# Second batch's weight rows handed over inside SBUF, late weight loads as steps of the first turns, new instruction orders

## Chip, cores and metric

The kernel runs on one core of one Trainium2 chip. The metric is device microseconds (us) of one execution; smaller is better.

## The reference, cut to what matters

Input x is 16 batches of 256 tokens by 256 channels. Four layers run one after the other on every batch, each steered by a 64-vector per batch:

```python
# A: adapter whose weights are generated per batch, then two norms and q, k, v
dW = (cond @ Wdd.T + bdd) * 0.1              # one 128x256 pair of matrices per batch
x  = x + relu(x @ (Wd + dWd).T + bd) @ (Wu + dWu).T + bu
x  = norm(x) * w + bias + tanh(...)          # layer 1
q, k, v = (norm(x) * g1 + b1) @ W_qkv.T      # layer 2, 16 heads of 16
# B: attention per head: softmax(q k^T / 4) v
# C: x + o @ W_o * a1;  then x + gelu_tanh(norm(x) @ W_f1) @ W_f2 * a2
# D: u = rms(x) @ up_w.T;  h = val * gelu(gate);  y = quant8(h) @ ternary(down_w).T + x
```

Batches do not depend on each other. The weights, and the generator of the adapter rows, are shared.

## The kernel before, in words

**Stages and turns.** The work of a batch is cut into stages A, B, C, D as above. In turn t the kernel does A of batch t, B of batch t-1, C of batch t-2 and D of batch t-3, so turns 0 to 18 cover 16 batches. The five instruction streams (SP issues every DMA; PE, ACT, DVE, POOL compute) are written out by hand: a text for each engine lists the order of the small steps ("A.v", "B.s0", "C.f1"), with `HEAD` for turns 0 to 5, `FULL` repeated for turns 6 to 12 and `TAIL` for the rest. Each step waits on semaphores that count the finished steps of other engines. An engine runs its own list strictly in order, so a step that waits holds all that stands behind it. PE is written `A.down, A.up, A.ht, A.q, A.k, A.v`; `B.s` are scores (each covers two of the eight head pairs), `B.m` the transposed maxima, `B.t` the transposed scores, `B.o` the outputs; `C.proj, C.ht, C.f0..3, C.g0..3, C.xt` are the output projection and the feed-forward; `D.u, D.qt, D.y` the last layer. Matmuls of A and C that need fp32 precision are done as three fp32r products of high and low parts (`three`, L504), hence every weight is split by ACT (`high_part`, L800) and DVE (`low_part`, L1040).

**Before the turns.** `hyper` (16 chunks of 1 MB, L344 and L370) streams through a ring of four buffers. PE turns each into rows of adapter weights for all 16 batches (L514), ACT and DVE in turn copy them into `gen` (L785, L981). As each chunk is ready SP copies the first batch's eight rows to `cur` (`first_rows`, L366). After the last one SP loads w_qkv (L399), stores all of `gen` to DRAM as `cur_scratch` in four transfers of 1 MB (L402), stores two constant planes (L404, L405), loads w_f1 (L408), waits for the four stores (L409), loads w_up (L410) over the place where it is split later, and starts the turns with `W.late` (w_f2 and w_down, L413 and L414). `gen` lies where the high part of w_up is written later.

**The adapter weights of a batch.** `combine(b)` on DVE (L1056, step `A.cur`) turns `cur` into `cur * 0.1 + base`. For b > 0 it waits for a load of `cur` from `cur_scratch` (L391), which SP issues in `A.load` together with the gates `tA` (L386) and the two layouts of x (L379, L380). In turn 0 DVE does `A.up A.lna A.lng A.ln W.qkv A.cur A.q`, so the q low part (L1132) stands behind `A.cur`, and PE's `A.v` (L504, twelve matmuls) waits for the q low part before it overwrites the bank.

**What else the steps touch.** `B.s0` of batch b needs the heads of q and k: ACT and DVE write high and low parts, SP stores them to `qk_scratch` (`A.qs`, `A.ks`, L420) and loads them back as heads 0 to 3 (`A.ql`, `A.kl`, L429). `C.g0` shares a bank with k and waits for the k low part (L1132). `C.f1` waits for the fourth maximum of stage B (L1140). DVE's `W.abs` (L1072) sums w_down.

The lines that cannot be said shorter, turn 0 and 1 of DVE:

```python
0: A.up A.lna A.lng A.ln W.qkv A.cur A.q 1: W.fa 0: A.k 1: A.up A.lna A.lng A.ln B.s0 B.s1 B.s2 B.s3 B.p0 B.m0
B.s4 B.s5 B.s6 B.s7 B.p1 B.m1 A.q W.up B.o1 A.k A.cur B.o3
```

Of the kernel before, what the change touches and what calls it, by code (L numbers as in the profile page):

```python
# [63 lines left out]
def at(steps, name, b):  # L64
# [13 lines left out]
        0: A.down A.up A.ht A.q A.k A.v 1: A.down A.up B.s0 B.s1 A.ht B.m0 B.s2 A.q B.s3 A.k B.m1 B.t0 B.t1 B.o0 B.t2 B.t3 B.o1 A.v 2: C.proj B.s0
# [1384 lines left out]
```

## Time and profile before

| | |
|---|---|
| time, median of 3 runs | 893.33 us (892.43 to 893.88) |
| time of the profiled execution | 892.32 us |
| its span, first to last instruction | 890.5 us |
| PE busy | 814.7 us, 91% |
| DVE, ACT, POOL busy | 551.0, 520.9, 235.1 us |
| all DMA engines busy (slices 2 and 4 of 40) | 382 and 409 GB/s |
| mean granted TensorE clock | 0.946 of full speed |
| chain that ended last, by engine | PE 80%, issue 8%, DVE 4%, DMA 3%, POOL 3% |

The span is shorter than the time by 1.8 us of start and end. Busy shares are means over stages of different kinds, so the views by stretch of time say more. A granted clock of 1.00 is 2.4 GHz and of 0.50 is 1.2 GHz.

### The profile page before, as it was taken

The numbers are of one execution on the slowest core, as the hardware profiler recorded it, in microseconds if no ns is written. First come the engines' busy times: TensorE is split into PE (matmuls) and PEld (weight loads), VectorE is DVE, ScalarE is ACT, GpSimd is POOL, SyncE is SP. The second block draws the span as 40 slices with busy tenths as digits, with TensorE's granted clock in tenths as the row PEclk, the third lists the DMA queues.
The fourth block names the chain that finished last, engine by engine and source line by source line (L and its number), as shares of the span: only waits on it lengthen the run. The fifth ranks groups of instructions, "written<-read, shape, count | busy, mean of one in ns | idle before, by whom it ended". The sixth has DMA issues, their size and how long they took to land.

```text
span 890.5 us, 15833 instructions
## 1 busy us (share of the span) xinstructions
PE 814.7 (91%) x5852; PEld 629.9 (71%) x5852; DVE 551.0 (62%) x1063; ACT 520.9 (58%) x808; POOL 235.1 (26%) x333
## 2 busy tenths in 40 slices
PE   6862477999999999999999999999999999999976
PEld 4212346777787878787878787878788787877665
DVE  1322567686767768585858585858585767656424
ACT  1112243566676758585867667666667676765642
POOL 1002213050505142423223140505050505030310
PEclk9855577999999999999999999999999999999999
DMA  9989733334242342424251514234242333230100
GB/s 346 382 309 409 234 130 112 117 113 150 71 163 72 110 135 85 160 85 161 84 162 52 178 64 151 94 117 129 102 139 102 119 114 107 102 101 3 31 13 12
DMA packets 56093, 118.48 MB, mean 133 GB/s; under 512 B 6000, under 2 KB 11504, under 8 KB 53312
## 3 DMA queue, kind: packets, MB, share of 16 engines
q1 hardware_dynamic: 56016, 117.48, 38.7%
q8 instruction: 46, 0.75, 0.3%
q14 instruction: 31, 0.25, 0.1%
HBM read 82.51 MB, written 34.16 MB: 131 GB/s over the span
## 4 chain that ended last, share of the span: by engine, by line
PE 80%; issue 8%; DVE 4%; DMA 3%; POOL 3%; ACT 1%; SPq 1%; POOLq 0%; DVEq 0%; ACTq 0%
PE bank L504 31%; PE bank L713 13%; PE pair_s L668 6%; PE pair_t L504 5%; PE bank L679 3%; PE bank L760 3%; PE pair_s L656 3%; PE pair_s L634 3%; DMA hyp<-in_hyper 2%; PE bank L572 2%; PE bank L578 2%; PE pair_t L656 2%; PE bank L752 2%; PE pair_t L634 1%; PE pair_t L514 1%
## 5 line engine op out<-in xcount | busy, mean ns | idle before, releaser
L713 PE MATMUL bank<-wf,G 128*128 128x256 f32 x512 | 126.6, 391 | 0.7 <-ACT G L885 0.5
L504 PE MATMUL bank<-wup_hi,hD_hi 128*128 128x512 f32 x256 | 110.2, 430 | 4.1 <-POOL hD_lo L1333 3.2
L1361 POOL TENSOR_TENSOR x<-x,xcr 128x512 f32<-128x512 f32 x16 | 20.8, 1301 | 335.4 <-DVE x L1198 335.4
L870 ACT ACTIVATE Pr<-pair_s 128x1024 f32<-128x1024 f32 x64 | 65.6, 1025 | 74.8 <-PE pair_s L656 74.8
L713 PEld LDWEIGHTS bank<-wf,G 128*128 128x128 f32 x512 | 92.2, 189 | 21.8 <-issue 5.8
L504 PE MATMUL bank<-wup_hi,hD_lo 128*128 128x512 f32 x256 | 101.6, 397 | 0.0
L504 PE MATMUL bank<-wup_lo,hD_hi 128*128 128x512 f32 x256 | 101.5, 396 | 0.0
L1140 DVE TENSOR_REDUCE nmax<-pair_s 128x4 f32<-128x1024 f32 x64 | 77.9, 1218 | 20.4 <-PE pair_s L634 20.3
L1164 DVE STREAM_TRANSPOSE oq<-pair_s 128x512 f32<-128x512 f32 x32 | 22.9, 717 | 88.7 <-PE pair_s L668 88.7
L1140 DVE TENSOR_REDUCE nmax<-pair_t 128x4 f32<-128x1024 f32 x64 | 77.4, 1210 | 0.0
L914 ACT ACTIVATE gl<-bank,rsD 128x512 f32<-128x512 f32 x64 | 43.8, 684 | 52.7 <-PE bank L504 52.5
L1208 DVE SCALAR_TENSOR_TENSOR hd<-bank,rsD,gl 128x512 f32<-128x512 f32 x64 | 47.8, 747 | 32.0 <-PE bank L504 30.8
L668 PE MATMUL pair_s<-Pr,Va 128*32 128x256 f32 x1024 | 65.1, 396 | 0.3 <-ACT Pr L870 0.2
L870 ACT ACTIVATE Pr<-pair_t 128x1024 f32<-128x1024 f32 x64 | 65.2, 1019 | 0.0
L504 PEld LDWEIGHTS bank<-wup_hi,hD_hi 128*128 128x128 f32 x256 | 48.3, 189 | 18.8 <-POOL hD_lo L1333 3.4
L504 PEld LDWEIGHTS bank<-wup_lo,hD_hi 128*128 128x128 f32 x256 | 48.4, 189 | 11.7
L504 PEld LDWEIGHTS bank<-wup_hi,hD_lo 128*128 128x128 f32 x256 | 48.6, 190 | 9.7
L668 PEld LDWEIGHTS pair_s<-Pr,Va 128*32 128x32 f32 x1024 | 29.6, 112 | 26.6 <-ACT Pr L870 8.4
L922 ACT ACTIVATE qT<-bank 128x1024 bf16<-128x1024 bf16 x32 | 32.8, 1024 | 23.6 <-PE bank L752 23.6
L504 PE MATMUL bank<-hA_hi,wqkv_hi 128*128 128x256 f32 x128 | 39.9, 312 | 3.4 <-POOL hA_lo L1333 3.4
L504 PE MATMUL bank<-hC_hi,wf_hi 128*128 128x256 f32 x128 | 38.1, 298 | 3.6 <-POOL hC_lo L1333 3.6
L1333 POOL TENSOR_TENSOR hA_lo<-hA,hA_hi 128x512 fp32r<-128x512 f32 x16 | 20.6, 1285 | 75.9 <-ACT hA_hi L849 75.9
(183 smaller groups left out, 2000.4 us busy)
## 6 DMA issues: line engine op xcount, KB each, us to landing
hyp<-in_hyper SPq DMA_DIRECT2D x16, 1024.0 KB, 8.6
Qp<-qk_scratch SPq DMA_DIRECT2D x64, 256.0 KB, 4.9
Kp<-qk_scratch SPq DMA_DIRECT2D x64, 256.0 KB, 4.7
qk_scratch<-q_hi SPq DMA_DIRECT2D x16, 512.0 KB, 2.8
qk_scratch<-k_hi SPq DMA_DIRECT2D x16, 512.0 KB, 3.4
tC<-rows_scratch SPq DMA_DIRECT2D x16, 384.0 KB, 4.3
xT_t<-in_xT SPq DMA_DIRECT2D x16, 256.0 KB, 4.3
x_t<-in_x SPq DMA_DIRECT2D x16, 256.0 KB, 4.5
```

Of the source, the lines that this page charges most:

```text
L504: mm = pe.matmul(dst, l, r, start=first and i == 0, stop=last and i == 2)
L634: mm = pe.matmul(pair[p % 2][:, half, r * L:(r + 1) * L], Qp[lo:lo + KR, 1 - par, p, r * P:(r + 1) * P], Kp[lo:lo + KR, 1 - par, p, :], st ...
L656: mm = pe.matmul(pair[p % 2][:, half, k * L:(k + 1) * L], Kp[lo:lo + KR, 1 - par, p, k * P:(k + 1) * P], Qp[lo:lo + KR, 1 - par, p, :], st ...
L668: mm = pe.matmul(bank[1][32 * j:32 * j + 32, (g % 2) * L:(g % 2 + 1) * L], Va[:, 1 - par, k, 4 * g + j, :], Pr[:, (2 * g + j // 2) % 4, j ...
L679: mm = pe.matmul(bank[5][:, r * D:(r + 1) * D], oT[:, k, r * P:(r + 1) * P], wo[:, k, :], start=k == 0, stop=k == KT - 1)
L713: mm = pe.matmul(bank[5][:, r * D:(r + 1) * D], G[:, k, r * P:(r + 1) * P], wf2[:, k, :], start=k == 0, stop=k == FT - 1)
L760: mm = pe.matmul(bank[6][:, 0:D], qT[:, k, :], wq3[:, k, :], start=k == 0, stop=k == FT - 1)
L870: act.activation(Pr[:, p % 4, :, :].rearrange("p a n -> p (a n)"), pair[p % 2][:, :, :].rearrange("p a n -> p (a n)"), ACT.Exp, scale=DH * ...
L914: act.activation(gl[:, n % 2, :], bank[6][:, :], ACT.Gelu, scale=rsD[:, 1, n // 2:n // 2 + 1]).then_inc(act_d, 1)
L922: act.activation(qT[:, :, :].rearrange("p k n -> p (k n)"), bank[7][:, :].bitcast(BF16), ACT.Copy).then_inc(act_d, 1)
L1140: dve.tensor_reduce(nmax[:, n % 2, :, p % GP, :], pair[p % 2][:, :, :].rearrange("p a (r n) -> p a r n", r=RT), AX.X, ALU.max, negate=True ...
L1208: dve.scalar_tensor_tensor(hd[:, (n % 2) * HALF:(n % 2 + 1) * HALF], bank[7][:, :], rsD[:, 1, n // 2:n // 2 + 1], gl[:, n % 2, :], ALU.mul ...
```

## The change

Four edits. (1) `first_rows` issues a second transfer for each chunk: the rows of batch 1 go from `gen` to a new SBUF tensor `second`, and `combine(1)` reads it, after PE's `A.up` of batch 0, which is the last reader of `cur`. The load of `cur` in `A.load` of turn 0 is dropped; that of turn 1 waits for the stores of `gen`. (2) w_qkv is loaded before the last four `first_rows`, not after them. (3) The stores and late loads become steps: `W.store` and `W.f` open turn 0, `W.up` stands behind `A.kl2` of turn 0, `W.late` behind `B.m0` of turn 1. The wait for all preparation before w_f1 is gone. (4) All five orders are new. The arithmetic is the same.

```diff
 HEAD = {
     "SP": """
-        0: W.late A.load A.qs A.ks A.ql0 A.kl0 A.ql1 A.kl1 A.kl2 A.kl3 A.ql2 A.ql3 1: A.load B.m0 A.qs B.m1 A.ql0 A.ql1 A.ks 2: C.tc 1: A.kl0 A.ql2
+        0: W.store0 W.f0 A.load A.qs A.ks A.ql0 A.ql1 A.kl0 A.kl1 A.ql2 A.kl2 W.up A.kl3 A.ql3 2: C.tc 1: A.load B.m0 W.late B.m1 A.qs A.ks A.ql0
...
     "PE": """
-        0: A.down A.up A.ht A.q A.k A.v 1: A.down A.up B.s0 B.s1 A.ht B.m0 B.s2 A.q B.s3 A.k B.m1 B.t0 B.t1 B.o0 B.t2 B.t3 B.o1 A.v 2: C.proj B.s0
-        A.down A.up B.s1 C.ht C.f0 C.f1 C.f2 W.abs B.m0 A.ht B.s2 C.f3 B.s3 A.q A.k B.m1 B.t0 A.v C.g0 B.t1 C.g1 B.o0 C.g2 B.t2 C.g3 B.t3 3: A.down
+        0: A.down A.up A.ht A.q A.k A.v 1: A.down A.up B.s0 B.s1 B.m0 A.ht B.s2 B.s3 A.q A.k B.m1 B.t0 B.t1 B.o0 B.t2 B.t3 B.o1 A.v 2: C.proj A.down
+        A.up B.s0 C.ht B.s1 W.abs C.f0 C.f1 C.f2 B.m0 A.ht B.s2 C.f3 B.s3 A.q A.k B.m1 B.t0 A.v C.g0 B.t1 C.g1 B.o0 C.g2 B.t2 C.g3 B.t3 3: A.down 2:
...
     "ACT": """
-        0: A.down W.qkv A.lnb A.ht W.fa A.q A.k A.v 1: A.down W.up A.lnb A.ht A.q A.k B.t0 B.t1 B.t2 B.t3 B.t4 B.t5 B.t6 B.t7 A.v 2: A.down C.lnb
+        0: W.qkv A.down A.lnb A.ht A.q A.k A.v W.fa 1: A.down A.lnb A.ht W.up A.q B.t0 B.t1 B.t2 B.t3 A.k B.t4 B.t5 B.t6 B.t7 A.v 2: A.down C.lnb
...
     "DVE": """
-        0: A.up A.lna A.lng A.ln W.qkv A.cur A.q 1: W.fa 0: A.k 1: A.up A.lna A.lng A.ln B.s0 B.s1 B.s2 B.s3 B.p0 B.m0 B.s4 B.s5 B.s6 B.s7 B.p1 B.m1
-        A.q W.up B.o1 A.k A.cur B.o3 2: C.proj B.s0 C.ln B.s1 A.up B.s2 A.lna A.lng B.s3 A.ln W.abs B.p0 B.m0 B.s4 B.s5 B.s6 B.s7 B.p1 B.m1 A.q A.k
+        0: W.qkv A.cur A.up A.lna A.lng A.ln A.q A.k 1: A.up A.lna A.lng A.ln B.s0 B.s1 B.s2 B.s3 B.p0 B.m0 W.fa B.s4 B.s5 B.s6 B.s7 B.p1 B.m1 A.q
+        A.cur W.up B.o1 A.k 2: W.abs 1: B.o3 2: C.proj C.ln A.up B.s0 A.lna B.s1 A.lng B.s2 B.s3 A.ln B.p0 B.m0 B.s4 B.s5 B.s6 B.s7 B.p1 B.m1 A.q
...
 FULL = {
     "SP": """
-        -1: A.kl2 A.ql1 A.kl3 A.ql2 A.ql3 D.y1 0: A.load B.m0 A.qs B.m1 D.y0 A.ks A.ql0 A.kl0 1: C.tc 0: A.kl1""",
+        -1: A.ql0 A.kl0 0: C.tc -1: A.kl1 D.y1 A.kl2 A.ql1 A.ql2 A.ql3 A.kl3 0: A.load B.m0 A.qs B.m1 D.y0 A.ks""",
     "PE": """
-        -1: B.m1 A.v B.t0 C.g0 B.t1 C.g1 D.qt1 B.o0 C.g2 B.t2 C.g3 B.t3 D.y1 B.o1 C.xt 0: A.down B.s0 C.proj D.u0 A.up D.u1 C.ht B.s1 D.u2 C.f0 C.f1
-        C.f2 B.m0 A.ht C.f3 B.s2 D.u3 B.s3 A.q D.qt0 A.k D.y0""",
+        -1: B.m1 A.v B.t0 C.g0 B.t1 C.g1 B.o0 D.qt1 C.g2 B.t2 C.g3 B.t3 D.y1 B.o1 C.xt 0: A.down B.s0 C.proj D.u0 A.up D.u1 C.ht B.s1 D.u2 C.f0 C.f1
+        C.f2 B.m0 C.f3 A.ht B.s2 D.u3 B.s3 A.q D.qt0 A.k D.y0""",
...
     "DVE": """
-        -1: C.g3 D.y1 B.o3 0: B.s0 C.proj B.s1 C.ln D.u0 A.up A.lna D.u1 A.lng B.s2 A.ln B.s3 B.p0 D.quant0 B.m0 D.u2 B.s4 B.s5 D.u3 B.s6 B.s7 B.p1
-        A.q A.k B.m1 D.quant1 A.cur D.y0 B.o1""",
+        0: D.u1 A.lng B.s2 B.s3 A.ln B.p0 D.quant0 B.m0 D.u2 B.s4 B.s5 D.u3 B.s6 B.s7 B.p1 A.q B.m1 A.cur A.k D.quant1 D.y0 B.o1 C.g3 D.y1 B.o3 1:
+        B.s0 C.proj B.s1 C.ln D.u0 A.up A.lna""",
     "POOL": """
-        0: A.down C.proj C.ln A.up C.ht A.lna A.ln A.ht C.g3 C.xt""",
+        0: A.ht C.g3 1: A.down 0: C.xt 1: C.proj C.ln A.up C.ht A.lna A.ln""",
...
+        second = staged("second", [P, 2 * D], F32, 2 * D)
...
                 sp.wait_ge(gen_act if c % 2 == 0 else gen_dve, c // 2 + 1)
                 sp.dma_start(cur[8 * c:8 * c + 8, :], gen[0:P:NB, c, :]).then_inc(first_in, 16)
+                sp.dma_start(second[8 * c:8 * c + 8, :], gen[1:P:NB, c, :]).then_inc(second_in, 16)
...
             def load_weights(b):
 
+                if b == 1:
+                    load_gates(b)
+                    return
                 sp.dma_start(cur[:, :], cur_rows[:, bass.ds(b, 1), :].rearrange("r o n -> (r o) n")).then_inc(cur_in, 16)
                 load_gates(b)
 
             load_rows(0)
+            sp.dma_start(wqkv_raw[:, :], w_qkv).then_inc(wqkv_in, 16)
             for c in range(NCH - 4, NCH):
                 first_rows(c)
             sp.wait_ge(rows_out, 16)
             load_gates(0)
-            sp.dma_start(wqkv_raw[:, :], w_qkv).then_inc(wqkv_in, 16)
...
-            sp.wait_ge(prep, len(PREP))
-            sp.dma_start(wf1_raw[:, :], w_f1).then_inc(wf1_in, 16)
-            sp.wait_ge(gen_out, 64)
-            sp.dma_start(wup_raw[:, :], w_up).then_inc(wup_in, 16)
+            def f1_rows():
+                sp.dma_start(wf1_raw[:, :], w_f1).then_inc(wf1_in, 16)
+
+            def up_rows():
+                sp.wait_ge(gen_out, 64)
+                sp.dma_start(wup_raw[:, :], w_up).then_inc(wup_in, 16)
...
                     elif (stage, what) == ("A", "load"):
 
+                        if t == 1:
+                            sp.wait_ge(gen_out, 64)
...
                 if b == 0:
                     dve.wait_ge(first_in, 16 * NCH)
+                elif b == 1:
+                    dve.wait_ge(second_in, 16 * NCH)
+                    dve.wait_ge(pe_a, at(PE_A, "up", 0))
                 else:
-                    dve.wait_ge(cur_in, 16 * b)
+                    dve.wait_ge(cur_in, 16 * (b - 1))
                 dve.wait_ge(dve_w, at(DVE_W, "base", 0))
-                dve.scalar_tensor_tensor(cur[:, :], cur[:, :], DELTA, base_c[:, :], ALU.mult, ALU.add).then_inc(cur_ready, 1)
+                dve.scalar_tensor_tensor(cur[:, :], second[:, :] if b == 1 else cur[:, :], DELTA, base_c[:, :], ALU.mult, ALU.add).then_inc(cur_ready, 1)
```

## Rows read from the trace of the kernel before

**Rows 1.** By stretch: length, busy PE, PEld, DVE, ACT, POOL; granted clock, DMA share, GB/s

```profile
57.00:60.00 3.00, 0.00 (x0) 0.00 (x0) 1.51 (x3) 0.00 (x0) 1.46 (x1) 0.50 0.16 49
...
83.00:86.00 3.00, 0.55 (x5) 0.34 (x3) 0.00 (x0) 0.84 (x2) 0.00 (x0) 1.00 0.96 401
84.00:93.00 9.00, 0.00 (x0) 0.00 (x0) 0.77 (x2) 0.43 (x2) 0.00 (x0) 0.62 0.97 366
...
140.00:150.00 10.00, 4.77 (x30) 3.17 (x29) 9.54 (x18) 4.50 (x7) 6.08 (x10) 0.88 0.00 1
...
185.00:850.00 665.00, 661.24 (x4979) 530.67 (x4978) 458.08 (x896) 450.89 (x700) 199.51 (x278) 1.00 0.33 107
850.00:890.50 40.50, 28.79 (x163) 22.59 (x161) 11.58 (x21) 12.07 (x20) 3.42 (x4) 0.96 0.04 14
```

**Rows 2.** Who waited for whom, 55 to 150 us: total, times, longest

```profile
DVE cur L1056 <- DMA cur<-cur_scratch: 20.2, 1, 20.2
...
PE bank L504 <- DVE q_lo L1132: 10.2, 1, 10.2
```

**Rows 3.** SP's DMA issues in time (start, length), and one group's min/median/max

```profile
58.70 0.43 SPq L399 DMA_DIRECT2D wqkv_raw<-in_w_qkv  x1
59.17 5.85 SPq L402 DMA_DIRECT2D cur_scratch<-gen  x4
...
76.14 0.33 SPq L410 DMA_DIRECT2D wup_raw<-in_w_up  x1
...
L366 SPq DMA_DIRECT2D cur<-gen x16: 563/580/725, 9.7 to 57.6; - x16
```

**Rows 4.** Timeline of turn 0 on DVE, POOL and ACT: start, length, instruction

```profile
67.16 0.19 POOL L1301 TENSOR_TENSOR rsA<-mvA,eps_ln 128x2 f32<-128x2 f32 x1 [7.86 <-DVE mvA L1099]
...
70.10 1.97 DVE L1040 TENSOR_TENSOR wqkv_lo<-wqkv_raw,wqkv_hi 128x1536 fp32r<-128x1536 f32 x1
70.41 1.71 POOL L1301 TENSOR_TENSOR rsA<-mvA,eps_ln 128x2 f32<-128x2 f32 x1
...
79.78 1.91 ACT L800 ACTIVATE wf_hi<-wf_raw 128x2048 fp32r<-128x2048 f32 x1 [2.56 <-DMA wf_raw<-in_w_f]
...
92.84 0.87 DVE L1132 SCALAR_TENSOR_TENSOR q_lo<-bank,small,q_hi 128x256 fp32r<-128x256 f32 x2
```

**Rows 5.** Chain of waits: PE pieces at the low and the high clock

```profile
93.76 2.94 PE bank L504 x12
...
100.08 2.09 PE bank L578 x4
...
199.78 1.42 PE bank L504 x12
```

**Rows 6.** Timeline: when batch 1's x had landed

```profile
94.65 2.38 POOL L1315 TENSOR_TENSOR x_t<-x_t,bu_t 128x512 f32<-128x512 f32 x1 [16.10 <-DMA x_t<-in_x]
```

**Rows 7.** Timeline of turn 1 on DVE and PE

```profile
93.62 2.28 DVE L1040 TENSOR_TENSOR wf_lo<-wf_raw,wf_hi 128x2048 fp32r<-128x2048 f32 x1
...
102.19 0.69 DVE L1106 TENSOR_TENSOR x<-bank,x_t 128x512 f32<-128x512 f32 x1 [5.50 <-PE bank L578]
...
112.45 0.28 DVE L1154 CAST mt<-pair_s 32x128 fp32r<-32x128 f32 x1 [0.49 <-PE pair_s L640]
...
117.58 1.23 DVE L1140 TENSOR_REDUCE nmax<-pair_s 128x4 f32<-128x1024 f32 x1 [1.51 <-PE pair_s L634]
...
121.15 0.50 PE L656 MATMUL pair_s<-Qp,Kp 64*128 64x256 f32 x4 [0.46 <-DVE mt L1154]
...
121.72 4.40 DVE L1040 TENSOR_TENSOR wup_lo<-wup_raw,wup_hi 128x4096 fp32r<-128x4096 f32 x1
...
127.83 0.72 DVE L1164 STREAM_TRANSPOSE oq<-pair_s 128x512 f32<-128x512 f32 x1 [1.71 <-PE pair_s L668]
```

**Rows 8.** Timeline of a middle turn, around the k low part

```profile
443.74 0.27 PE L640 MATMUL pair_s<-small,parts 128*32 128x128 f32 x1
...
443.84 0.88 DVE L1132 SCALAR_TENSOR_TENSOR k_lo<-bank,small,k_hi 128x256 fp32r<-128x256 f32 x2 [0.84 <-ACT k_hi L856]
...
446.03 1.35 PE L713 MATMUL bank<-wf,G 128*128 128x256 f32 x5
```

More of the change, by code:

```diff
@@ L77 @@
+        A.kl0 A.ql1 A.kl1 A.ql2 A.kl2 A.ql3 A.kl3 2: A.load B.m0 A.qs B.m1 A.ks A.ql0 A.kl0 A.ql1 3: C.tc 2: A.kl1 A.ql2 A.kl2 A.kl3 A.ql3 3: A.load
+        B.m0 A.qs B.m1 D.y0 A.ql0 A.ql1 A.ks A.ql2 A.kl0 A.kl1 4: C.tc 3: A.kl2 A.ql3 4: A.load 3: A.kl3 4: B.m0 A.ks B.m1 A.qs A.kl0 3: D.y1 4:
+        A.ql0 5: C.tc 4: A.kl1 D.y0 D.y1 A.ql1 A.kl2 A.ql2 A.kl3 A.ql3 5: A.load B.m0 A.qs B.m1 D.y0 A.ks""",
     "PE": """
[L78 removed]
@@ L101 @@
+        A.up C.ht A.lna A.ln A.ht C.g3 6: A.down 5: C.xt 6: C.proj C.ln A.up C.ht A.lna A.ln""",
 }
@@ L122 @@
+        D.y1 A.kl2 A.ql1 A.ql2 A.ql3 A.kl3 14: A.load B.m0 A.qs B.m1 D.y0 A.ks A.ql0 A.kl0 A.ql1 15: C.tc 14: D.y1 A.ql2 A.ql3 A.kl1 A.kl2 A.kl3 15:
+        B.m0 A.qs B.m1 D.y0 A.ks A.ql0 A.kl0 A.kl1 16: C.tc 15: A.ql1 A.kl2 A.kl3 D.y1 A.ql2 A.ql3 16: B.m0 B.m1 D.y0 D.y1 17: C.tc D.y0 D.y1 18:
+        D.y0 D.y1""",
     "PE": """
-        12: B.m1 A.v B.t0 C.g0 B.t1 C.g1 D.qt1 B.o0 C.g2 B.t2 C.g3 B.t3 D.y1 B.o1 C.xt 13: A.down B.s0 C.proj D.u0 A.up D.u1 C.ht B.s1 D.u2 C.f0
-        C.f1 C.f2 B.m0 A.ht C.f3 B.s2 D.u3 B.s3 A.q D.qt0 A.k D.y0 B.m1 A.v B.t0 C.g0 B.t1 C.g1 D.qt1 B.o0 C.g2 B.t2 C.g3 B.t3 D.y1 B.o1 C.xt 14:
@@ L398, in _, with store_rows @@
             load_gates(0)
-            sp.dma_start(wqkv_raw[:, :], w_qkv).then_inc(wqkv_in, 16)
-            for i in range(4):
-                sp.dma_start(cur_scratch[4 * i:4 * i + 4].rearrange("c p n -> p c n"), gen[:, 4 * i:4 * i + 4, :]).then_inc(gen_out, 16)
-            sp.wait_ge(zero, 6)
-            sp.dma_start(qk_scratch[0, :, 3, :], ys[:, :, :].rearrange("p r n -> p (r n)")).then_inc(planes_out, 16)
-            sp.dma_start(qk_scratch[1, :, 3, :], Kp[:, 1, 0:2, :].rearrange("p c n -> p (c n)").bitcast(F32)).then_inc(planes_out, 16)
-            sp.wait_ge(prep, len(PREP))
-            sp.dma_start(wf1_raw[:, :], w_f1).then_inc(wf1_in, 16)
-            sp.wait_ge(gen_out, 64)
-            sp.dma_start(wup_raw[:, :], w_up).then_inc(wup_in, 16)
+            def store_rows():
+                for i in range(4):
+                    sp.dma_start(cur_scratch[4 * i:4 * i + 4].rearrange("c p n -> p c n"), gen[:, 4 * i:4 * i + 4, :]).then_inc(gen_out, 16)
+                sp.wait_ge(zero, 6)
+                sp.dma_start(qk_scratch[0, :, 3, :], ys[:, :, :].rearrange("p r n -> p (r n)")).then_inc(planes_out, 16)
+                sp.dma_start(qk_scratch[1, :, 3, :], Kp[:, 1, 0:2, :].rearrange("p c n -> p (c n)").bitcast(F32)).then_inc(planes_out, 16)
+            def f1_rows():
[3 more added lines that the diff above has]
+                sp.dma_start(wup_raw[:, :], w_up).then_inc(wup_in, 16)
             def late_weights():
@@ L441, in turn @@
                     if stage == "W":
-                        late_weights()
+                        {"store": store_rows, "f": f1_rows, "up": up_rows, "late": late_weights}[what]()
                     elif (stage, what) == ("A", "qs"):
```

81 lines of the change are left out of this document (39 added, 42 removed).

## The prediction

> **What bounds the kernel now.** I read the busy time by stretch first [rows 1]. From 185 to 850 us PE is busy for 661.2 of 665 us at the full clock: turns 3 to 16 are PE's own work. An order that moves other engines about can win at most the 3.8 us of idle time there, and can only lose more if it makes PE wait. The idle time lies at both ends. At the start, 84 to 93 us has no matmul at all while the DMA engines are 97% busy, and 140 to 150 us has PE busy for half. At the end, 850 to 890.5 us is 11.7 us idle.
>
> Then the waits [rows 2]. PE waited 10.2 us in one piece, for the q low part of batch 0. That is a cheap instruction (0.87 us [rows 4]), held in DVE's list behind `combine(1)`, which itself waited 20.2 us for `cur` from `cur_scratch`. SP's issues say why that load is late [rows 3]: w_qkv and four 1 MB stores of `gen` go out from 58.7 us, SP waits until 76.14 us for the stores, then w_up, w_f2 and w_down (4 MB) are issued ahead of `cur`. So 4 MB of late weights stand between a finished row in `gen` and its use, and PE pays for it. This wait is what the change takes away.
>
> **The change, part by part.** Instants are those of the old trace; a minus is earlier.
>
> *Row transfers.* Sixteen more issues at 0.58 us [rows 3] on SP, one for each chunk. SP's loop has room: a chunk takes some 2.6 us, of which SP used about 1. The ring of chunks is DMA-bound, so what counts is the added traffic: 16 KB beside 1 MB is 1.6%, some 0.6 us over the loop of 45 us. Bounds: 0, and 1.3 us if eight rows keep only half of the engines busy. I take +0.6.
>
> *w_qkv earlier.* It now stands ahead of the last rows of batch 0. Between 57 and 60 us the DMA engines are 16% busy [rows 1], so most of its 0.8 MB (1.9 us at some 400 GB/s, the table's rate of full DMA engines) fills a hole, and the hole is where the last `cur` rows land. Bounds 0 and 1.9; I take +0.3, because the rows are issued about when it is nearly through.
>
> *combine(1).* It stands ahead of `A.up` on DVE and waits for the same PE step, so all of it is on the path: +0.7 (a 128x512 element pass on DVE is 0.69 us, `x` in [rows 7]).
>
> *W.qkv on DVE.* It used to start at 70.10 us, and POOL's 128x2 add at 70.41 took 1.71 us where the same add took 0.19 at 67.16 [rows 4]. Now it runs while PE does `A.down`, and POOL is free: -1.5. The Trainium skill (SBUF — State Buffer, section "SBUF: two separate sides") says that a DVE operation with two SBUF inputs and a GpSimd operation exclude each other for a whole instruction; the trace agrees, as the add ended with the DVE pass (72.1). The same rule speaks against the new place of `W.fa`, which now meets POOL's `hA_lo` of turn 1: there it could delay that subtraction by up to the pass's 2.28 us [rows 7]. I count nothing, since PE's `A.q` is by then held by other work (below).
>
> Together turn 0 reaches `A.q` at +0.6 +0.3 +0.7 -1.5 = +0.1.
>
> *The wait.* The q low part now follows q at once, some 83.5 us, when PE ends k: -10.2 for `A.v` [rows 2]. Beside that, PE's clock had gone to 1.00 by 83 us and fell while PE was idle: the mean over 84 to 93 is 0.62 [rows 1]. `A.v` will run without a gap behind k: twelve matmuls take 1.42 us at 2.4 GHz and 2.94 at 1.2 [rows 5], so -1.5. `A.down` gains nothing, as ACT now does `W.fa` (1.91 us [rows 4]) ahead of its relu. `A.up` (2.09 us [rows 5]) may halve or not: 0 to -1.0, I take -0.5. The x0 of batch 1, at 102.19 us before, comes at about 90.
>
> *Is the data there?* The x of batch 1 landed at 94.6 us [rows 6], behind the late weights. It is now issued some 72 us, behind 6.5 MB counted from 59 us; at 400 GB/s that is 78 us and with latency about 80 to 82. PE wants it at 85.6. Slack 4. Of the moved transfers w_up is issued behind six head loads at 90 us and ahead of the last two; ACT wants it at 100, and the heads behind it are wanted at 104, some 6 us after they land. w_f2 and w_down go out near 102 and are wanted at 118 or later. Stores of q and k find a short queue. All this I cost at nothing; the cover is the slack named.
>
> *Turn 1, DVE and PE.* Before, x0 to the first transposed score took 121.15 - 102.19 = 19.0 us [rows 7]. DVE now has `W.fa` (2.28 us) between the first maxima and pair 4. It used to wait 0.98 there and 1.51 before pair 6, because `A.q` stood ahead of `B.s3` on PE [rows 7]; so DVE's own chain does not grow. But PE now does `A.q` and `A.k` after `B.s3`, hence after the maximum of pair 5: 10.5 (the copy of the first maxima ends at 112.73 [rows 7]) + 2.3 (`W.fa`) + 2.4 (pairs 4, 5) + 0.8 = 16.0; `A.q` at the low clock 2.9, `A.k` at the high 1.4, then 0.9 for the maxima: 21.2. That is +2.2. Bounds: +0.8 with both at 2.4 GHz, +3.7 with both at 1.2. `W.up` (4.40) follows with `A.cur` ahead of it; DVE idled 1.71 before the output transpose at 127.83 [rows 7], so 0.69 more fits.
>
> *Turn 2.* `W.abs` leaves the busiest stretch of DVE (9.54 of 10 us in 140 to 150 [rows 1]) for one where DVE waits. In exchange `C.ln` comes ahead of `B.s0` and waits for POOL with DVE idle, so the fourth maximum, for which `C.f1` waits, is about as late as before: +0.3 (0 to +1).
>
> *The middle.* PE's work is the same and fills the time: 0, at best -0.5. *The end:* in turn 17 `C.ht` comes ahead of `D.u2`; that saves one short wait and adds another, and the last 27 us are one chain of the same steps: 0, bounds -1 and +1.
>
> Sum: 0.1 - 10.2 - 1.5 - 0.5 + 2.2 + 0.3 = **-9.6 us**. The profiled execution took 892.32 us, so 882.7; the median of the runs is 1.0 above it, which gives 883.7. I say 883.2.
>
> **The rivals.**
>
> *More than that (879.5).* The clock, once up at 83 us, stays up through turn 1, so that `A.up`, the scores and `A.q` run at 2.4 GHz: -0.5 and -1.5 and some in `B.o`, together -13. For it: PE's longest hole is gone. Against it: in the old trace the clock fell inside turn 1 as well, between score groups, and those gaps stay.
>
> *Less than that (887).* Another wait takes over in turn 1: the heads, or x of batch 1 behind the stores. If the 6.5 MB move at 320 GB/s instead of 400, they end 4 us later, the slack is used up, and a further 1 to 2 us are lost; with `A.k` at the low clock (+1.5) and 1.9 for w_qkv ahead of the first rows, the gain shrinks to 5 or 6.
>
> *Hidden anyway (893).* The change does not do what it says if something as late as `cur` stands behind it in turn 1. For that, the heads of batch 0 would have to be 10 us late again; but they were stored and loaded in 8 us, and only after the q low part.
>
> *Slower (899).* One mechanism: the k low part in every middle turn. It now stands behind `B.m1` and `A.cur` on DVE, while PE's `C.g0` waits for it. In the middle turn PE's maxima end at 444.01 us, then 0.2 + 0.6 + 0.9 puts the k low part at 445.8, and `C.g0` starts at 446.03 [rows 8]. The margin is 0.25 us in each of ten turns. The gain of 9.6 is eaten when it is overrun by 1 us in each; 899 needs 1.6. Against it: every length in that sum is a row, and DVE has idle time in each turn.
>
> **How the numbers follow.** Forecast (-8 to -12) 0.60; more 0.13; less 0.19; hidden 0.04; slower 0.04. A measurement of this kernel can tell about 0.2%, or 1.8 us. Faster by over 0.2%: 0.92; within: 0.04; slower: 0.04. The range 879 to 888 holds the forecast, most of "more" (low bounds of the clock terms) and most of "less".
>
> **What would show it.** No wait of DVE on `cur` in turn 0; `A.v` at about 83.5 us with the clock at 1.00; POOL's add near 0.2 us; x0 of batch 1 near 90; the first transposed score of batch 0 near 111; `C.f0` near 140 instead of 149.5; then 185-to-850-like PE busy of over 99%. Wrong: PE waits of over 2 us on heads or x in turn 1, a wait of `C.g0` on the k low part that recurs in each turn, or the chunk loop ending more than 1.5 us later.

## The result, and the profile after

The changed kernel took **890.17 us** (median of 20 runs, 888.61 to 892.01); the kernel before, run beside it, 891.84 (20 runs). The ratio is 0.9978, with a 95% interval of 0.9968 to 0.9988: a gain of 2 us where 9.6 were forecast, and the time lies outside the range. The profiled execution took 888.86 us, with a span of 887.0 at a mean granted clock of 0.948.

First who waited for whom in the changed kernel, 56 to 100 us (total, times, longest), to be held against [rows 2]:

```profile
POOL rsA L1316 <- DVE mvA L1114: 20.0, 2, 10.1
ACT x L844 <- POOL rsA L1323: 16.8, 2, 9.2
DVE q_lo L1147 <- ACT q_hi L868: 10.8, 1, 10.8
```

DVE's 20.2 us for `cur` and PE's 10.2 us for the q low part are gone. What DVE waits for now is ScalarE's q, the next step of the chain. One wait is new: PE starts the scores of batch 0 at 95.82 us, after 2.93 us of waiting for its heads, and over 2 us was a sign of being wrong in the prediction. It costs little, since DVE was busy with the norms of batch 1 meanwhile and takes the first maximum 4.8 us behind x0 in both kernels. The same is seen in the timeline of DVE and POOL in turn 0, against [rows 4] and [rows 7]:

```profile
63.86 0.69 DVE L1071 SCALAR_TENSOR_TENSOR cur<-cur,base_c 128x512 f32<-128x512 f32 x1 [2.99 <-DMA cur<-gen]
...
69.47 0.69 DVE L1071 SCALAR_TENSOR_TENSOR cur<-second,base_c 128x512 f32<-128x512 f32 x1 [3.25 <-issue]
...
75.17 0.19 POOL L1316 TENSOR_TENSOR rsA<-mvA,eps_ln 128x2 f32<-128x2 f32 x1
...
85.75 0.88 DVE L1147 SCALAR_TENSOR_TENSOR q_lo<-bank,small,q_hi 128x256 fp32r<-128x256 f32 x2 [10.81 <-ACT q_hi L868]
...
92.93 0.69 DVE L1121 TENSOR_TENSOR x<-bank,x_t 128x512 f32<-128x512 f32 x1 [3.74 <-PE bank L590]
```

Batch 1's rows are combined at 69.47 us, as soon as PE's `A.up` of batch 0 is through, without a wait for data; POOL's add is 0.19 us and no longer 1.71, and x0 of batch 1 comes at 92.93 where it came at 102.19: 9.3 us earlier. So the middle of the argument holds. The stretches of [rows 1] show that it does not hold at either end:

```profile
57.00:60.00 3.00, 1.94 (x8) 0.20 (x8) 0.42 (x1) 0.15 (x1) 0.00 (x0) 0.50 0.91 357
...
84.00:93.00 9.00, 7.15 (x36) 6.06 (x35) 1.82 (x5) 4.43 (x7) 0.71 (x1) 0.81 0.61 214
...
185.00:850.00 665.00, 659.72 (x4973) 527.73 (x4972) 450.37 (x879) 456.20 (x704) 194.17 (x269) 1.00 0.33 106
850.00:887.00 37.00, 26.13 (x131) 19.64 (x128) 11.67 (x21) 9.48 (x15) 3.42 (x4) 0.85 0.04 15
```

84 to 93 us, empty before, now has PE busy for 7.15 us. But at 57 to 60, where the chunk loop was over, PE still does the last chunk's eight matmuls with the DMA engines 91% busy. And the last stretch has the clock at 0.85, not 0.96. The chain of waits shows how far the loop slipped:

```profile
57.57 1.98 PE pair_t L526 x8
...
60.29 3.37 DMA cur<-gen
...
63.86 0.70 DVE cur L1071
...
64.70 1.52 PE bank L584 x3
```

In the kernel before, the same four pieces start at 54.89, 57.61 (and take 1.87), 59.67 and 60.51 us. The first matmul of the turns is **4.2 us later**, where the prediction had 0.9.

The table gives marks of every kernel of this study, from the profiled execution of each: the start of the last chunk's matmuls (L), the first matmul of `A.down` of turns 0, 1 and 3 (D0, D1, D3), the time from D3 to D5, and from `A.down` of turn 15 to the end of the span (E). "Change" is the ratio of the medians.

| kernel | median us | change [95%] | L | D0 | D1 | D3 | D3 to D5 | E |
|---|---|---|---|---|---|---|---|---|
| before | 891.6 to 892.3 | | 54.89 | 60.51 | 97.47 | 177.59 | 96.97 | 148.9 |
| changed | 890.17 | 0.9978 [0.9968, 0.9988] | 57.57 | 64.70 | 89.69 | 169.22 | 97.57 | 153.2 |
| tail_old | 885.81 | 0.9927 [0.9914, 0.9940] | 57.26 | 64.69 | 89.31 | 171.64 | 97.61 | 150.0 |
| no_second | 885.56 | 0.9923 [0.9910, 0.9936] | 53.38 | 59.86 | 83.65 | 165.68 | 97.57 | 153.2 |
| qkv_late | 892.23 | 1.0000 [0.9988, 1.0011] | 57.33 | 62.95 | 92.05 | 173.88 | 97.60 | 153.1 |
| extra_rows | 896.83 | 1.0041 [1.0028, 1.0054] | 57.46 | 63.08 | 100.90 | 182.64 | 96.97 | 149.5 |
| head_only | 881.92 | 0.9887 [0.9866, 0.9907] | 55.73 | 61.47 | 85.67 | 165.09 | 96.97 | 150.2 |
| q_first | 882.35 | 0.9889 [0.9869, 0.9910] | 54.70 | 61.21 | 85.44 | 167.62 | 96.98 | 149.3 |
| tail_old16 | 887.96 | 0.9955 [0.9938, 0.9971] | 57.24 | 64.77 | 89.98 | 169.68 | 97.59 | 150.6 |
| rows_late | 887.24 | 0.9946 [0.9927, 0.9966] | 53.62 | 59.96 | 85.46 | 171.85 | 96.95 | 148.9 |
| extra_tiny | 894.03 | 1.0014 [1.0001, 1.0026] | 54.78 | 60.45 | 98.24 | 178.15 | 97.01 | 150.1 |
| extra_wide | 894.30 | 1.0016 [1.0003, 1.0029] | 54.87 | 60.51 | 98.44 | 179.49 | 96.99 | 149.5 |
| before_load | 882.27 | 0.9887 [0.9870, 0.9903] | 53.87 | 59.48 | 84.99 | 169.25 | 97.00 | 149.5 |

D1 to D3 differs by 2.8 us among kernels with the same orders there (79.5 in the changed kernel, 82.3 in tail_old; between 110 and 120 us the granted clock was 0.93 in the one and 0.67 in the other), so one profile is no proof for a term of 2 us in turns 1 and 2. L also differs by 2.3 us among kernels with the same loop. But L, D3 to D5 and E fall into groups with no overlap, and carry the argument. A difference between the medians of two kernels of this table is good to some 1.5 us, by the intervals of their ratios.

### The profile page after: what moved, and what is told of

The parts are those of the page before. It is cut to its first block, busy times and chain, and to the rows that moved or that the text cites. A ratio compares the mean times of both kernels' runs of the same rounds, so it can differ in the third digit from the quotient of the medians.

```text
span 887.0 us, 15853 instructions
## 1 busy us (share of the span) xinstructions
PE 815.2 (92%) x5852; PEld 628.6 (71%) x5852; DVE 552.5 (62%) x1063; ACT 526.5 (59%) x812; POOL 232.1 (26%) x333
## 4 chain that ended last, share of the span: by engine, by line
PE 80%; issue 7%; DMA 5%; DVE 3%; POOL 2%; ACT 2%; SPq 1%; POOLq 0%; DVEq 0%; ACTq 0%
PE bank L516 32%; PE bank L725 13%; PE pair_s L680 6%; PE pair_t L516 5%; PE bank L772 3%; PE bank L691 3%; PE pair_s L668 3%; PE pair_s L646 3%; DMA hyp<-in_hyper 2%; PE bank L764 2%; PE pair_t L668 2%; PE pair_t L646 2%; PE bank L584 1%; PE bank L590 1%; DMA x_t<-in_x 1%
## 5 line engine op out<-in xcount | busy, mean ns | idle before, releaser
L1348 POOL TENSOR_TENSOR hA_lo<-hA,hA_hi 128x512 fp32r<-128x512 f32 x16 | 20.6, 1288 | 92.9 <-ACT hA_hi L861 92.9
L844 ACT ACTIVATE xc<-xc,rsC 128x256 f32<-128x256 f32 x32 | 17.5, 594 | 41.0 <-POOL rsC L1323 41.0
```

## The experiments

### First round: undo one part each

**tail_old**: the changed kernel with the old orders of all engines from turn 14 on. TensorE's turn 16, as an example (the three dots stand for equal steps):

```diff
-16: B.s0 C.proj D.u0 B.s1 D.u1 C.ht D.u2 C.f0 C.f1 C.f2 B.m0 B.s2 D.u3 B.s3 D.qt0 C.f3 D.y0 B.m1 B.t0 C.g0 B.t1 C.g1 ...
+16: C.proj B.s0 D.u0 D.u1 C.ht B.s1 D.u2 C.f0 C.f1 C.f2 B.m0 C.f3 B.s2 D.u3 B.s3 C.g0 D.qt0 C.g1 B.m1 B.t0 C.g2 B.t1 D.y0 ...
```

> The changed kernel with the orders of the kernel before from turn 14 on. In the profiles the changed kernel is 7.8 us ahead when A.down of batch 15 starts and 3.5 us ahead at the end. Theory 'tail order': the new order of turns 15 to 17 costs most of the 4.3 us lost there, so this kernel keeps 6 to 8 us of the lead: ratio to before about 0.992 (884 to 886 us), 3 to 4 us below the changed kernel. Rival 'clock by chance': the loss is that the last matmuls fell to 1.2 GHz in the profiled execution (880 to 884 us); then this kernel is within 1.5 us of the changed one, ratio about 0.997, and A.down of batch 15 to the end takes 149 to 153 us from run to run whatever the order.

Measured: 885.81 us, 4.4 below the changed kernel, and E 150.0 where that has 153.2. The new order costs the last turns over 3 us, at a granted clock in the last 10 us that is about the same in both (0.62 and 0.61). That is a term the prediction had at 0, with bounds of 1 us.

**no_second**: no transfers of batch 1's rows; `cur` of batch 1 comes from `cur_scratch` as before, but still ahead of w_up, w_f2 and w_down.

```diff
-                sp.dma_start(second[8 * c:8 * c + 8, :], gen[1:P:NB, c, :]).then_inc(second_in, 16)
...
-                        if t == 1:
+                        if t == 0:
                             sp.wait_ge(gen_out, 64)
```

On DVE, `A.cur` of turn 0 stands behind `A.ln` again.

> The changed kernel without the sixteen transfers of batch 1's rows: cur of batch 1 is loaded from cur_scratch again, but in A.load of turn 0, after the wait for the stores and ahead of w_up, w_f2 and w_down; combine(1) is back behind A.ln. Theory 'row transfers load the chunk loop': the last chunk's matmuls start at 54.9 us again instead of 57.6 and the first A.down at 60.5 to 61.5 instead of 64.7; cur lands about 80.5 us, before the q low part could run, so A.v does not wait; 3 to 4 us faster than the changed kernel, ratio to before about 0.994. Rival 'the SBUF handover is what wins': cur lands behind the stores at 84 us or later, A.v waits 2 us or more, and the kernel is no faster than the changed one (ratio 0.998 or more).

Measured: 885.56 us, 4.6 below the changed kernel. Without the direct rows the last chunk comes at 53.38 and the first `A.down` at 59.86. The rows out of DRAM were early enough for everything that PE waits for: DVE waited 7.11 us for `cur` and had combined it by 77.3 us, 3 us before ScalarE's q was there. So the direct path, the part that gave the change its name, costs 4.6 us and saves none. Some 0.65 of that is `combine(1)`, which is off PE's path again: `A.down` to `A.q` of turn 0 takes 16.6 us, not 17.24.

**extra_rows**: the kernel before, with the sixteen row transfers added and not used.

```diff
                 sp.dma_start(cur[8 * c:8 * c + 8, :], gen[0:P:NB, c, :]).then_inc(first_in, 16)
+                sp.dma_start(second[8 * c:8 * c + 8, :], gen[1:P:NB, c, :]).then_inc(second_in, 16)
```

> The kernel before with the sixteen transfers of batch 1's rows added and their data not used. My prediction costed them at 0.6 us (0 to 1.3). The profiles differ by 2.7 us at the last chunk. Theory 'row transfers load the chunk loop': chunk pitch in the last eight chunks rises from 2.6 to about 3.0 us, the first A.down comes 2.5 to 3.5 us later and the total rises by as much: ratio 1.003 to 1.004. Rival 'another part of the change slows the loop': the loop ends within 1 us of before and the ratio is 1.000 to 1.001.

Measured: 896.83 us, ratio 1.0041, last chunk at 57.46. The price shows by itself, without any other part of the change: 2.6 us in the loop, and 4.5 between the medians. Where some of the rest lies is seen in the third round.

**qkv_late**: the changed kernel with w_qkv behind the last rows and gates, as before.

```diff
-            sp.dma_start(wqkv_raw[:, :], w_qkv).then_inc(wqkv_in, 16)
             for c in range(NCH - 4, NCH):
                 first_rows(c)
             sp.wait_ge(rows_out, 16)
             load_gates(0)
+            sp.dma_start(wqkv_raw[:, :], w_qkv).then_inc(wqkv_in, 16)
```

> The changed kernel with w_qkv issued behind the last rows and gates, as before. The last rows of batch 0 took 3.4 us from issue to landing in the changed kernel, 1.9 us in the one before. Theory 'w_qkv stands ahead of the last rows': landing is back at about 2 us and the first A.down is 1 to 1.5 us earlier; w_qkv lands some 2 us later, which ACT and DVE take before A.q without a wait; total 1 us below the changed kernel. Rival 'the second transfer or the queue is at fault': no change of the first A.down, total within 0.5 us, or up to 1 us slower because w_qkv's low part meets A.up on DVE.

Measured: 892.23 us, 2 slower than the changed kernel: a miss. The first `A.down` did come 1.75 us earlier, so the early w_qkv does delay the last rows. But DVE's and ScalarE's new orders begin turn 0 with `W.qkv`. With the weight late, ScalarE's relu of `A.down` stood behind it and PE waited 5.21 us for that, so `A.down` of turn 1 came 2.4 us later. The order and the place of the transfer are one decision.

### Second round: add the parts up, and look inside them

**head_only**: no_second, with the old orders of all engines from turn 3 on.

> Second batch's rows loaded as one transfer from the scratch as in no_second, the new orders for turns 0 to 2 alone, the old orders of all engines from turn 3 on. Theory (three separate costs: 2.7 us in the loop and 1.5 at the landing, 0.6 us in turns 3 and 4, 3.2 to 4.3 us in the tail): A.down(3) to A.down(5) 96.97 us, A.down(15) to the end 149 to 150 us, A.down(1) near 83.7 us, so the time is some 4 us under both tail_old (885.8) and no_second (885.6): 881 to 882.5 us, ratio 0.987 to 0.989. Rival (the two gains are the same microseconds, or the clock falls wherever the earlier work has left it): 884.5 to 886 us, ratio 0.992.

Measured: 881.92 us, ratio 0.9887, as the theory had it. D3 to D5 is 96.97 again and E 150.2. The costs of loop and orders are separate: 4.6 + 4.4 is 9.0, and taking both away brought 8.3.

**q_first**: head_only with one step moved on TensorE.

```diff
-1: ... B.s2 B.s3 A.q ...
+1: ... B.s2 A.q B.s3 ...
```

> head_only with one step moved: TensorE takes A.q of turn 1 ahead of B.s3 and no longer behind it. Theory (the order term of +2.2 us in turn 1 is real): from x0(1) to B.t0 of turn 1 19 us where no_second has 21.8, and A.down(2) 2 us earlier than head_only; time 1.5 to 2.5 us under head_only. Rival (pairs 6 and 7 come later and VectorE waits for them, or TensorE gets as late to B.t0 by another way): x0 to B.t0 over 21 us, time within 0.7 us of head_only.

Measured: 882.35 us, no difference, and x0 of batch 1 (88.7) to the first transposed score (110.16) takes 21.5 us, where head_only has 20.6. The rival was right: PE does `A.q` first, and DVE waits 2.89 us ahead of pair 6 for its scores.

**tail_old16**: the changed kernel with the old orders from turn 16 on only (on SP, also for the head loads of batch 15).

> The changed kernel with the old orders from turn 16 on (turns 0 to 15 as changed). Theory (the loss at the end lies in turns 16 and 17, where the new order runs C.g0 and C.g1 no longer between B.s3 and B.m1 and ScalarE changes tables four times more): A.down(15) to C.proj(16) stays 48.4 us, C.proj(16) to the end falls from 104.7 to about 102, time 887 to 888 us, ratio 0.995. Rival (the loss is made by turn 15's order, which leaves A.v behind): C.proj(16) to the end stays at 104 to 105 us, time 889.5 to 890.5.

Measured: 887.96 us; this gains 2.2 us, half of what tail_old gained. From `A.down` of turn 15 to `C.proj` of turn 16 it takes 47.93 us (changed kernel 48.45, tail_old 47.29), to `C.proj` of turn 17 42.77 (44.14, 42.79), and from there to the end 59.93 (60.6, 59.94). So theory and rival are both half right: by these marks the orders of turns 14 and 15 cost 0.6 us (47.93 less 47.29), those of turn 16 0.5 ahead of its `C.proj` and 1.4 behind it, those of turn 17 0.7. The stretches from `C.proj` of turn 16 on, 22 us each, show it for turn 16. In the changed kernel:

```profile
782.40:804.40 22.00, 21.02 (x127) 16.93 (x128) 16.24 (x25) 11.52 (x19) 5.74 (x8) 1.00 0.07 26
```

and in tail_old16:

```profile
780.97:802.97 22.00, 21.94 (x139) 18.57 (x139) 15.32 (x26) 13.45 (x23) 6.32 (x9) 1.00 0.23 76
```

With the old order PE is busy 21.94 of 22 us and has done twelve matmuls more by then. It has `C.g0` and `C.g1` between `B.s3`, `D.qt0` and `B.m1` as cover while DVE and ScalarE finish the maxima; the new order has `C.f3` and `D.y0` there, and `C.g0` and `C.g1` behind `B.t0`. Who waited for whom on PE, 782 us to the end of the changed kernel, says the same in small pieces:

```profile
PE bank L734 <- POOL x L1376: 1.5, 2, 1.2
...
PE bank L516 <- POOL hC_lo L1348: 0.5, 2, 0.3
...
PE pair_s L646 <- DVE mt L1169: 0.5, 1, 0.5
PE pair_t L668 <- ACT Pr L882: 0.4, 1, 0.4
```

None of the last three is among PE's waits of the kernel before in these turns. They add up to 1.4 us, less than the loss. That the cover is the cause was not tried step by step; that the orders are, was.

**rows_late**: head_only's orders, but batch 1's rows inside SBUF, all sixteen transfers behind the loop and the gates. One thing more differs: SP issues w_f behind `A.load` of turn 0, not ahead of it.

```diff
             load_gates(0)
+            for c in range(NCH):
+                sp.dma_start(second[8 * c:8 * c + 8, :], gen[1:P:NB, c, :]).then_inc(second_in, 16)
...
-        0: W.store0 W.f0 A.load ...
+        0: W.store0 A.load W.f0 ...
```

> head_only but with the second batch's rows moved inside SBUF as in the changed kernel, all sixteen transfers issued behind the first gates, after the last chunk's, and none in the loop. Theory (the sixteen transfers cost what they cost because they share the loop's queues): last chunk's matmuls start at 54 to 55 us as before the change, first A.down at 60 to 61, VectorE has the rows by 80 us and waits for nothing, A.down(1) 83.5 to 85; time within 1 us of head_only. Rival (their cost is their own, 16 x 0.3 to 0.4 us of queue work wherever they stand, and delays w_f, w_up or the stores): A.down(1) 2 us or more later than head_only, time 1.5 to 3 us above it.

Measured: 887.24 us, 5.3 above head_only. The loop is fast again (last chunk 53.62, first `A.down` 59.96) and DVE waits for no row; yet the price is back, and larger. The issues on SP's queue (start, length) show it:

```profile
56.57 9.67 SPq L418 DMA_DIRECT2D second<-gen  x16
66.28 3.53 SPq L422 DMA_DIRECT2D cur_scratch<-gen  x4
...
72.68 1.23 SPq L400 DMA_DIRECT2D tA<-rows_scratch  x1
...
76.56 1.24 SPq L428 DMA_DIRECT2D wf_raw<-in_w_f  x1
```

Sixteen issues hold SP for 9.67 us, 0.60 each, and the stores of `gen` and w_f stand behind them. In those us the chip moves almost nothing (last two columns: DMA share and GB/s):

```profile
60.00:62.00 2.00, 2.00 (x4) 1.11 (x4) 1.76 (x1) 0.07 (x1) 0.00 (x0) 0.50 0.08 25
62.00:64.00 2.00, 1.44 (x4) 1.18 (x4) 0.00 (x0) 0.47 (x1) 0.00 (x0) 0.50 0.11 33
```

ScalarE then waits 4.30 us for w_f ahead of its relu, and x0 of batch 1 comes at 92.80, not 88.91. But w_f is issued at 76.56 us, where head_only has 66.95, and 3.9 us of that (72.68 to 76.56) are the three issues of `A.load` that were put ahead of it. So this kernel shows that the loop is fast without the transfers and that sixteen issues hold SP for 9.67 us; how much of the 5.3 us they cost, and how much the later w_f, is open. The rival had the place of the price wrong, since `A.down` of turn 1 itself was not later, only all behind it.

### Third round: what makes a row transfer dear, and which part earned the gain

**extra_tiny** and **extra_wide**: as extra_rows, with one row of 2 KB a transfer, and with 16 KB in 128 pieces of 128 bytes.

```diff
+                sp.dma_start(second[8 * c:8 * c + 1, :], gen[1:2, c, :]).then_inc(second_in, 16)
```

```diff
+                sp.dma_start(second[:, 32 * c:32 * c + 32], gen[:, c, 0:32]).then_inc(second_in, 16)
```

> The kernel before with sixteen more transfers in the loop, unused, each of one row of 2 KB where extra_rows had eight rows. Theory A (a transfer costs by being one: issue, descriptors and completion in a full queue): as dear as extra_rows, last chunk's matmuls at about 57.4 us, chunk pitch 3.0 us, 895.5 to 897 us, ratio 1.004. Theory B (the eight rows load few of the sixteen DMA engines, so 16 KB costs 0.3 to 0.4 us of the loop and 2 KB a eighth of that): last chunk near 55.2, pitch 2.6 to 2.7, time within 1 us of before, ratio 1.000 to 1.001.

> The same with sixteen unused transfers of 16 KB each, as many bytes as in extra_rows, but as 128 pieces of 128 bytes over all partitions. Theory A (per transfer): as extra_rows, 895.5 to 897 us. Theory B (few engines loaded): all sixteen engines share the piece, so the cost is that of the added bytes or of the many small pieces: 1 MB in 64 KB a engine becomes 65, +0.1 us a chunk, 893 to 895 us; above 898 us the number of pieces is what counts.

Measured: 894.03 and 894.30 us, ratios 1.0014 and 1.0016, where extra_rows has 1.0041. The last chunk is at 54.78 and 54.87, as in the kernel before. 44 to 52 us in extra_rows:

```profile
44.00:48.00 4.00, 2.37 (x12) 0.20 (x8) 0.69 (x1) 0.60 (x1) 0.00 (x0) 0.50 1.05 357
48.00:52.00 4.00, 2.60 (x12) 0.40 (x16) 0.00 (x0) 0.60 (x1) 0.00 (x0) 0.50 1.00 365
```

and in extra_wide, which moves as many bytes:

```profile
44.00:48.00 4.00, 3.02 (x16) 0.33 (x16) 0.69 (x1) 0.00 (x0) 0.00 (x0) 0.50 1.00 385
48.00:52.00 4.00, 2.71 (x12) 0.20 (x8) 0.55 (x1) 0.60 (x1) 0.00 (x0) 0.50 1.05 395
```

So the 2.6 us in the loop is neither the price of one more issue (extra_tiny has as many) nor that of 16 KB more (extra_wide has them). It belongs to the form. What the form was, the packet counts of the kernels tell, here before, extra_rows, extra_tiny and extra_wide:

```profile
DMA packets 56093, 118.48 MB, mean 133 GB/s; under 512 B 6000, under 2 KB 11504, under 8 KB 53312
DMA packets 56350, 118.75 MB, mean 133 GB/s; under 512 B 6129, under 2 KB 11633, under 8 KB 53569
DMA packets 56605, 118.52 MB, mean 133 GB/s; under 512 B 6512, under 2 KB 12016, under 8 KB 53824
DMA packets 58397, 118.75 MB, mean 133 GB/s; under 512 B 8304, under 2 KB 13808, under 8 KB 55616
```

A transfer of extra_rows made 16 packets (one of the 257 is an instruction queue's), half of them under 512 bytes: eight of 2 KB with data and eight small ones. One of extra_tiny made 32 (512 more in all), every one under 512 bytes: its 2 KB row was not moved as one piece, but in sixteen of 128 bytes, with sixteen small ones. One of extra_wide made 144: 128 with data and again sixteen small ones. So where the second transfer costs nothing in the loop it has sixteen small packets, and where it is dear it has eight. That fits half of theory B, eight of the sixteen DMA engines getting all the extra work. But no view shows single engines; pieces of 2 KB against pieces of 128 bytes would fit as well; and if the other engines stood idle until the slowest was through, the DMA share should fall, while it is 1.00 to 1.05 in extra_rows. That the form is dear is shown; why is argued.

Both kernels are also some 2 us above before in the median and not in the loop. Half of it can be found. `A.down` of turn 0 starts at 60.45 and 60.51 us, as before (60.51), but that of turn 1 at 98.24 and 98.44, where before has 97.47. The last extra issue stands ahead of the stores, and in these kernels `cur` still waits for the stores. In extra_tiny, to be held against [rows 3] and the 92.23 us at which DVE combined `cur` before:

```profile
59.81 5.78 SPq L417 DMA_DIRECT2D cur_scratch<-gen  x4
93.00 0.69 DVE L1073 SCALAR_TENSOR_TENSOR cur<-cur,base_c 128x512 f32<-128x512 f32 x1 [20.99 <-issue]
```

The stores go out 0.6 us later and `cur` is ready 0.8 us later. extra_rows has the same 0.9 us between `A.down` of turns 0 and 1 (37.8, not 36.96). The rest is open, and at 0.1% cannot be told.

**before_load**: the kernel before, with SP's list alone changed: batch 1's rows, gates and x ahead of w_up, and w_f2 and w_down behind the heads of turn 0.

```diff
-            sp.wait_ge(gen_out, 64)
-            sp.dma_start(wup_raw[:, :], w_up).then_inc(wup_in, 16)
+            def up_rows():
+                sp.dma_start(wup_raw[:, :], w_up).then_inc(wup_in, 16)
...
+                            if t == 0:
+                                sp.wait_ge(gen_out, 64)
                             load_weights(upcoming)
...
-        0: W.late A.load A.qs A.ks A.ql0 A.kl0 A.ql1 A.kl1 A.kl2 A.kl3 A.ql2 A.ql3 1: A.load
+        0: A.load W.up A.qs A.ks A.ql0 A.kl0 A.ql1 A.kl1 A.kl2 A.kl3 A.ql2 A.ql3 W.late 1: A.load
```

> The kernel before with one thing changed on SP alone: the second batch's rows, gates and x go out behind the stores and ahead of w_up, and w_f2 and w_down behind the last heads of turn 0. Orders of the other engines are the old ones. Theory (the late load is what the change was worth, the orders are needed only in turns 1 and 2): DVE waits under 1 us for cur in place of 20.2, A.down(1) near 85 to 88 us, and the time 4 to 8 us under before, ratio 0.991 to 0.995; head_only (881.9) keeps 2 us or more over it, since ScalarE's W.up comes right behind A.down of turn 1 and waits for w_up, and the heads stand behind it. Rival (the old order has no use for early rows, since every engine meets w_up or the heads next): time within 2 us of before.

Measured: **882.27 us**, ratio 0.9887: 10 us under the kernel before and 7.9 under the changed one, and no different from head_only (881.92). I had expected head_only to keep 2 us over it. SP's issues and DVE's timeline in this kernel:

```profile
58.15 6.05 SPq L415 DMA_DIRECT2D cur_scratch<-gen  x4
...
75.39 0.32 SPq L404 DMA_DIRECT2D cur<-cur_scratch  x1
...
77.18 0.43 SPq L424 DMA_DIRECT2D wup_raw<-in_w_up  x1
```

```profile
79.90 0.69 DVE L1072 SCALAR_TENSOR_TENSOR cur<-cur,base_c 128x512 f32<-128x512 f32 x1 [8.85 <-DMA cur<-cur_scratch]
81.60 0.88 DVE L1148 SCALAR_TENSOR_TENSOR q_lo<-bank,small,q_hi 128x256 fp32r<-128x256 f32 x2 [1.01 <-ACT q_hi L872]
```

DVE still waits 8.85 us for `cur`, more than the 1 I had expected, but it is through by 80.6, a microsecond before ScalarE's q is there. The wait costs PE nothing. That the heads now stand behind w_up does show: PE waits 6.99 us for them at 94.78. Yet the medians are equal. In the profiles head_only is 3.6 us ahead, but before_load was profiled in the slowest of its five executions (884.63 us, median 882.27) and head_only in one below its median (880.97), so whether the early heads are worth anything is open.

## Why the prediction was wrong

By its own steps, in their order.

*Row transfers (+0.6, bounds 0 and 1.3): the step that failed first.* It priced 16 KB by its bytes, as 1.6% of a chunk. The thirteen kernels fall into two groups: the eight without a second transfer of eight rows have the last chunk at 53.38 to 55.73 us, mean 54.5; the five with it at 57.24 to 57.57, mean 57.4. That is +2.9, and the same bytes in another form cost nothing in the loop. The bound of 1.3, for "eight rows keep only half of the engines busy", doubled the price of the bytes; what was measured is over twice that bound, so even if half of the engines is what happens, it does not give the size.

*w_qkv earlier (+0.3, bounds 0 and 1.9).* From the last chunk's matmuls to the first `A.down` it is 5.6 us in all six kernels with w_qkv behind, 5.74 to 6.5 in the four with it ahead, and 7.1 to 7.5 in the three with it ahead and both row transfers. So +0.7 alone (mean 6.3), and +1.7 together with the rows (mean 7.4). The hole at 57 to 60 us, which was to hide it, had been filled by the loop itself, which ran 2.7 longer. Both terms: 0.9 forecast, 4.2 in the profile. The rows and `combine(1)`'s place are 4.6 between the medians of no_second and the changed kernel, both with w_qkv early.

*combine(1) and POOL (+0.7, -1.5): right.* `A.down` to `A.q` of turn 0 takes 17.24 us (64.70 to 81.94); in the kernel before 18.19 (60.51 to 78.70). -0.95 against -0.8; by no_second, which has 16.6, `combine(1)` is 0.65 of it. The port rule of the Trainium skill (SBUF — State Buffer, section "SBUF: two separate sides") is borne out by 0.19 us against 1.71 for the same add. The changed kernel also shows it the other way round, in turn 1: POOL's `x_t` add runs from 110.41 us for 1.27, and the 128x16 subtraction that DVE starts at 110.45 takes 1.27 us, where it took 0.18 eight us earlier. PE was busy with `A.q` and `A.k` until 112.8, so this costs nothing here.

*The wait, `A.v` and `A.up` (-12.2): right.* From `A.down` of turn 0 to that of turn 1 it is 25.0 us, not 36.96: -12.0, of which -0.95 is the step above; -11.0 remains against -11.7 for the wait and `A.v`. From there to x0 of batch 1 it is 3.24 us, not 4.72: `A.down` and `A.up` of turn 1 both run at the high clock (1.10 and 1.13 us, not 2.05 and 2.08), -1.5 where -0.5 was forecast. Together -12.5. before_load, which takes away this wait and moves w_f2 and w_down back, gains 10.0 over the whole kernel. The wait was the whole worth of the change, and its size was well read.

*Turn 1's order (+2.2): right, link by link.* x0 of batch 1 to the first transposed score takes 20.6 us, not 19.0, so +1.6. `A.q` starts 15.8 us behind x0 (16.0 in the prediction's sum), `A.q` and `A.k` take 4.1 (4.3), and PE goes on without a gap to the maxima. In one profile this is not exact: other kernels with the same order there have up to 22.0. But q_first shows that the place of `A.q` alone is not what costs: ahead of `B.s3` it holds up pair 6 instead. What both orders share, and the kernel before has not, is `W.fa` (2.27 us) between the first maxima and pair 4; it was not tried by itself.

*Turn 2 (+0.3).* From the first transposed score to `C.f0` it is 27.3 us, not 28.4, and `C.f0` starts at 140.90, near the 140 that was named. Within the scatter of D1 to D3 this is as forecast.

*The middle (0): nearly.* The pitch of the middle turns is 46.7 us before and after, so the slower rival, the k low part in each turn, did not occur. The join from the first turns costs 0.6 in turns 3 and 4 (97.6 against 97.0 in every kernel, by its order there).

*The end (0, bounds -1 and +1): the second step that failed.* The order tables of turns 15 to 17 were compared in one place, turn 17's `C.ht`. The loss lies in turns 15 (0.6), 16 (1.9) and 17 (0.7), together 3.2 us with tail_old's clock as low at the end, and 4.4 between the medians of the changed kernel and tail_old. The other 1.1 us by which E grew (4.3 in all) goes with the clock: the kernel before was profiled with 1.00 in its last 10 us, the changed one with 0.62 (PE busy for 3.81 and 4.96 us). Of the ten kernels with the old orders there, three fell to 0.61 to 0.63 (E 150.0 to 150.2), one to 0.92, and six stayed at 1.00 (E 148.9 to 149.5); all three with the new orders fell. So the clock falls under either order; whether it falls more often under the new one, three profiles cannot tell.

The sum by medians: +4.6 (rows), -10.0 (the wait and what hung on it, by before_load), +4.4 (orders of the end) is -1.0, where -1.7 was measured between the medians and -2 by the ratio; the small terms are within what is left. The forecast of -9.6 took in the gain in full and two losses at almost nothing. The rival "less" had the right direction, but looked for the loss in turn 1's data: x was there in time, and the 2.93 us for the heads were covered. Of the signs named for being wrong, the one that counted is the chunk loop ending over 1.5 us later; it ended 2.7 later.

## What to carry to other kernels

When the profile shows one late load, first try to change its place in the issue list alone: here that was worth 10 us, and the other edits of the change, a new path for the data and new orders, took back 8. Do not price an extra transfer in a saturated queue by its bytes alone: as eight rows of 2 KB it cost nearly five times what its share of the bytes would have it cost, and as 128-byte pieces nothing in the loop; and each issue held SP for 0.5 to 0.6 us, ahead of all that stood behind it. And an instruction order that is new as a whole needs each stage's marks set beside the old ones; a stage that "has the same steps" can cost 3 us.
